# One fetch moved ahead of two others on the loading queue of a fused attention and expert layer

## The reference, cut to what matters

```
x (64*32, 256) as (latent, batch);  ctx (32, 1601, 256)
n  = layernorm(x)
q  = n @ Wq + bq ;  k = ctx @ Wk + bk ;  v = ctx @ Wv + bv        # cross attention
x  = x + gamma * layernorm(softmax(q @ k.T) @ v + n) + beta
x  = x + attention_2(layernorm(x); w_q, b_q, w_kv, w_out, b_out)  # 16 heads over the latents
h  = layernorm(x)
x  = x + sum over the top 2 of 16 experts (gate, up, down) + shared expert
```

## Time and profile before

| | |
|---|---|
| three timed runs | 533.95, 536.94, 537.23 us, median 536.94 |
| the profiled execution | 534.44 us, its span in the trace 532.3 us |
| TensorE busy | 494.5 us (93% of the span) |
| VectorE busy | 386.8 us (73%) |
| ScalarE, GpSimd busy | 219.3 us (41%), 203.7 us (38%) |
| mean granted TensorE clock | 0.984 of full speed |
| DMA traffic | 108.92 MB, mean 205 GB/s |

### The profile page before, as it was taken

How to read it: one execution, slowest core, us unless ns; L and a number is a source line. 1 busy time by engine, 2 the same in 40 slices (tenths; PEclk the granted TensorE clock), 3 DMA queues, 4 the chain that set the end, 5 groups by cost and what they waited for, 6 DMA issues and landing times.

```text
span 532.3 us, 14494 instructions
## 1 busy us (share of the span) xinstructions
PE 494.5 (93%) x5028; PEld 345.4 (65%) x5029; DVE 386.8 (73%) x1053; ACT 219.3 (41%) x656; POOL 203.7 (38%) x344
## 2 busy tenths in 40 slices
PE   7999969999999999999989999999998979999990
PEld 6866536665666656666655667766654548888870
DVE  4897489999789978898743478898766605555764
ACT  3444404533334444344432356666540025555520
POOL 5002130312211221222221476776776625665550
PEclk9999979999999999999999999999999989999997
DMA  8986968686998878885303899720022235555748
GB/s 290 377 313 175 364 195 279 194 265 227 339 299 298 285 232 270 277 273 204 112 21 107 245 309 325 238 90 1 33 75 86 90 109 150 155 158 141 239 100 246
DMA packets 67610, 108.92 MB, mean 205 GB/s; under 512 B 8371, under 2 KB 49381, under 8 KB 67560
## 3 DMA queue, kind: packets, MB, share of 16 engines
q1 hardware_dynamic: 60872, 97.57, 58.1%
q0 software_dynamic: 3792, 8.43, 4.5%
q10 hardware_dynamic: 2896, 2.23, 1.3%
HBM read 85.31 MB, written 24.85 MB: 207 GB/s over the span
## 4 chain that ended last, share of the span: by engine, by line
PE 71%; DMA 9%; DVE 6%; POOL 5%; issue 3%; SPq 2%; ACT 2%; ACTq 1%; POOLq 0%; DVEq 0%
PE banks L1206 15%; PE banks L1180 15%; PE banks L1590 8%; POOL rows_by_expert L773 4%; PE banks L1602 4%; PE banks L1194 3%; PE banks L1219 3%; DMA ring<-in_ctx_dram 3%; PE banks L1584 2%; DMA bk_col<-in_L_xattn_bk_dram 2%; PE banks L1317 2%; PE banks L1369 2%; PE banks L1227 2%; PE banks L1324 2%; PE banks L1340 1%
## 5 line engine op out<-in xcount | busy, mean ns | idle before, releaser
L1714 DVE STREAM_TRANSPOSE ctxT<-ring 128x832 f32<-128x832 f32 x124 | 118.2, 1009 | 8.8 <-DMA ring<-in_ctx_dram 8.5
L1180 PE MATMUL banks<-ctxT,qT_all 32*64 32x416 f32 (+2 forms) x2048 | 96.3, 507 | 6.3 <-DVE ctxT L1714 4.7
L1206 PE MATMUL banks<-ring,prob 128*64 128x256 f32 (+1 forms) x832 | 93.6, 381 | 0.7 <-ACT prob L888 0.7
L1180 PEld LDWEIGHTS banks<-ctxT,qT_all 32*64 32x64 f32 x2048 | 56.4, 133 | 37.0 <-issue 13.1
L1206 PEld LDWEIGHTS banks<-ring,prob 128*64 128x64 f32 (+1 forms) x832 | 58.6, 137 | 31.5 <-issue 4.2
L672 POOL TENSOR_TENSOR var<-mv,eps 128x1 f32<-128x1 f32 x32 | 6.2, 193 | 151.6 <-DVE mv L1755 97.1
L807 POOL DMA_INDIRECT expert_out<-prob,dest x47 | 46.3, 985 | 39.6 <-issue 21.6
L1590 PE MATMUL banks<-ring,ctxT 128*128 x188 | 49.4, 386 | 0.0
L901 ACT ACTIVATE prob<-banks,negmax 128x416 f32<-128x416 f32 (+2 forms) x80 | 41.0, 532 | 19.5 <-DVE negmax L1736 19.5
L1726 DVE TENSOR_REDUCE blockmax<-banks 128x1 f32<-128x416 f32 (+1 forms) x64 | 32.3, 566 | 20.5 <-PE banks L1180 20.5
L720 POOL TENSOR_TENSOR ctxT<-ctxT,k_mask 128x1088 f32<-128x1088 f32 x16 | 33.1, 2069 | 24.9 <-ACT ctxT L997 24.9
(11 more groups left out here) (279 smaller groups left out, 957.0 us busy)
## 6 DMA issues: line engine op xcount, KB each, us to landing
ring<-in_ctx_dram SPq DMA_DIRECT2D x48, 1024.0 KB, 8.5
qT_all<-q_by_pair SPq DMA_DIRECT2D x56, 128.0 KB, 8.0
rows_by_expert<-blank SPq DMA_DIRECT2D x8, 774.0 KB, 6.8
ctxT<-rows_by_expert SPq DMA_DIRECT2D x47, 129.0 KB, 2.1
mid<-stage SPq DMA_DIRECT2D x30, 128.0 KB, 2.3
ring<-in_ctx_dram SPq DMA_DIRECT2D x16, 130.0 KB
ctxT<-mid SPq DMA_DIRECT2D x16, 128.0 KB, 3.8
qT_all<-mid SPq DMA_DIRECT2D x16, 128.0 KB, 4.5
```

Source lines behind the costliest of these rows:

```text
L1180: last = pe.matmul(S[a][64 * b:64 * b + 64, 0:KW[a]], q_rep[mine, r, c, 64 * b:64 * b + 64], ctxT[mine, c, b, 0:KW[a]], start=c == 0, stop ...
L1206: last = pe.matmul(U[64 * b:64 * b + 64, 0:D], probT[0:rows, k, 64 * b:64 * b + 64], ring[0:rows, r, b, k, :], start=k == 0, stop=k == KT)
L1714: dve.transpose(ctxT[:, c].rearrange("p b (k j) -> p (b k) j", j=Q), ring[:, r].rearrange("p b k c -> p (b k) c")[:, :, columns(c):columns ...
```

## The change

Three things are written differently on SyncE's queue, and nothing on another engine. For pair 3, `follow` now issues the context before the queries (`late=0`; the number says which of the two semaphores `q_stored` the queries wait for). The six vector loads, which stood ahead of `follow` of pair 3, stand behind it. `follow` of pair 4 is as it was.

```diff
             load_q(DIRECT, DIRECT)
-            for to, of in ((bv_b, "L0_xattn_bv"), (gamma_b, "L0_xattn_gamma"), (beta_b, "L0_xattn_beta")):
-                sp.dma_start(to[:, :], t[of].partition_broadcast(P)).then_inc(weights_loaded, 16)
-            sp.dma_start(bq2_col[:, :], t["L0_attn_b_q"].rearrange("(p a) -> p a", a=1)).then_inc(weights_loaded, 16)
-            sp.dma_start(bout_b[:, :], t["L0_attn_b_out"].partition_broadcast(P)).then_inc(weights_loaded, 16)
-            sp.dma_start(rbias_b[:, :], t["L0_ffn_router_bias"].partition_broadcast(P)).then_inc(weights_loaded, 16)
-            def follow(i, r, stores=True, late=False):
+            def follow(i, r, stores=True, late=None):
 
                 sp.wait_ge(block_used, (i - RING + 1) * BLOCKS)
-                if not late:
+                if late is None:
                     load_q(i, r)
                 if stores:
                     store(i - RING - 2)
                 for g in range(len(KPARTS)):
                     sp.wait_ge(pv_done, (i - RING) * len(KPARTS) + (g + 1))
                     load_part(i, r, g)
-                if late:
-                    sp.wait_ge(q_stored[1], 16 * QUADS)
+                if late is not None:
+                    sp.wait_ge(q_stored[late], 16 * QUADS)
                     load_q(i, r)
 
-            follow(RING, 0, stores=False)
-            follow(RING + 1, 1, stores=False, late=True)
+            follow(RING, 0, stores=False, late=0)
+            for to, of in ((bv_b, "L0_xattn_bv"), (gamma_b, "L0_xattn_gamma"), (beta_b, "L0_xattn_beta")):
+                sp.dma_start(to[:, :], t[of].partition_broadcast(P)).then_inc(weights_loaded, 16)
+            ...
+            follow(RING + 1, 1, stores=False, late=1)
```

More of the change, by code:

```diff
@@ L500, in follow @@
                     load_part(i, r, g)
-                if late:
-                    sp.wait_ge(q_stored[1], 16 * QUADS)
+                if late is not None:
+                    sp.wait_ge(q_stored[late], 16 * QUADS)
                     load_q(i, r)
-            follow(RING, 0, stores=False)
-            follow(RING + 1, 1, stores=False, late=True)
+            follow(RING, 0, stores=False, late=0)
+            for to, of in ((bv_b, "L0_xattn_bv"), (gamma_b, "L0_xattn_gamma"), (beta_b, "L0_xattn_beta")):
+                sp.dma_start(to[:, :], t[of].partition_broadcast(P)).then_inc(weights_loaded, 16)
+            sp.dma_start(bq2_col[:, :], t["L0_attn_b_q"].rearrange("(p a) -> p a", a=1)).then_inc(weights_loaded, 16)
+            sp.dma_start(bout_b[:, :], t["L0_attn_b_out"].partition_broadcast(P)).then_inc(weights_loaded, 16)
+            sp.dma_start(rbias_b[:, :], t["L0_ffn_router_bias"].partition_broadcast(P)).then_inc(weights_loaded, 16)
+            follow(RING + 1, 1, stores=False, late=1)
             for i in range(RING + 2, 8):
```

## The result

The changed kernel takes 530.96 us (median of 20 runs, 528.96 to 534.85), the kernel before in the same rounds 536.58 us (532.63 to 537.65). The ratio is 0.9921, with a 95% interval of 0.9902 to 0.9941, so 4.2 us less. The means of the 20 and 20 executions differ by 4.6 us (531.4 against 536.0) and the medians by 5.6 us: each kernel's times spread unevenly over 5 to 6 us, which moves a median more than the ratio, and I go by the ratio. On another chip the same file measured 0.9933 (0.9903 to 0.9962), where one execution of ten (539.94 us) was in the chip's slower state and is left out. The forecast was 528.8 us and 6.8 us less: the direction and the place were right, the size was 1.6 times what the ratio shows. The forecast gave 0.55 to a gain of over 1% and 0.41 to one within 1%; at 0.8% the second came.

What follows compares the result with a forecast made beforehand. Pair 3's late context was taken to stall VectorE, then TensorE. Gain of 7.1 us less 0.3 for thin cover, 6.8 net, from the 535.6 us mean gave 528.8 us; 80% range 526 to 534.

Steps and rivals of the forecast that it cites:

- Steps 1 and 2: Pair 3's context on SyncE's queue: first part issued at 41.41, 5.67 us earlier, and landing at 55.3 us.
- step 2: Landing of pair 3's context: 3.28 MB plus 0.9 MB at 356 GB/s, 11.7 us, queries dropped from the traffic ahead.
- Step 3: Pair 3's scores on TensorE end at 70.8 instead of 77.88: 7.1 us gained, 4.7 stall and 2.2 slow clock.
- Steps 4 and 5: Transfers moved behind: vectors land at 59.8, free for pair 3's scores up to 60.3; 0.3 us charged for thin cover.
- step 4: Moved transfers: queries land by 56.8 at no cost; vectors cost 3.0 us of full DMA time and land at 59.8.
- Step 6: What is late next: pair 4's context, issued at 58.28 as before, wanted at 73.5, all traffic ended by about 72.
- third rival: The next stage gives it back: pair 4's queries come at 84.3, 4 us lost, gain 2.8, 532.8 us; chance 0.08.
- vectors late: Vectors queue behind 3.8 MB and land at 62 to 66; gain 3.4 us at 64, 532.2 us; chance 0.23.
- v + 10.5: End of pair 3's scores if the vectors land at time v and GpSimd's additions hold them; free up to v = 60.3.
- Context late: Pair 3's transfers land at 57.3 to 62; at 60 the gain is 4.4 us, 531.2 us; chance 0.09.
- slower: Vectors so late that TensorE, VectorE and GpSimd stand; with pair 4's context ahead, v = 69.0 and 537.2 us; chance 0.05.

Runs made afterwards that it cites:

- vec_only: Kernel before with only the six vector loads moved behind pair 3's context, pair 3's queries still ahead of it; ratio 0.9906 against the kernel before.
- awake: Kernel before, SyncE's order unchanged, with 20 extra 128x128 matmuls on TensorE between the fifth and sixth score blocks of pair 3; ratio 0.9984.
- big_behind: Kernel before with only the four 128 KB vector loads behind pair 3's context, the two small-row loads still ahead; ratio 0.9920.
- small_behind: Kernel before with only the two small-row loads (bq2_col, router bias) behind pair 3's context, the four 128 KB loads ahead; ratio 0.9996.
- five_too: Changed kernel with pair 5's context also issued ahead of the store of pair 0 and pair 5's queries; ratio 0.9894 against the kernel before.

## Why the prediction was right, and where it was too large

**Steps 1 and 2** held. The context landed 14.0 us after its first issue (42.64 to 56.67); step 2 had 13.9. The working was less good than the sum, and that the two agree to 0.1 us is partly luck: the rate of 413 GB/s ended at 52 us, by when 3.6 MB had moved since 42 us (362 GB/s), that is 3.1 MB beside pair 2's queries, and the landing of the 3.28 MB came only at 56.67. What kept it back is not shown. The 0.9 MB of step 2 are in the trace of before: from 62.5 to 72 us it has 2.90 MB in all, 0.52 of them the store that ScalarE's queue began at 62.12, so about 0.9 of pair 4's 3.28 MB had moved when pair 3's context landed. That the last of several DMA engines lagged was my reading; no trace shows them singly. Step 2's price for the queries, which it dropped from the traffic, was not borne out by vec_only.

**Step 3** held: 70.8 forecast for the end of pair 3's scores, 71.50 measured on a run that was 0.5 us late from the start. Its split was 4.7 of stall and 2.2 of clock. The 2.2 of clock is the 4.44 us that blocks 5 to 7 took at a granted clock of 0.50, less 2.2 us, three fifths of the 3.72 us of the five blocks ahead; that was an estimate, and no run shows it. awake puts the clock at 1.8: behind such a stall the three blocks take 2.6 us at a granted clock of 1.00 too, near VectorE's pace of 2.88 us for its three blocks.

**Steps 4 and 5** held to 0.4 us: vectors at 60.15 for a forecast of 59.8 and a limit of 60.3. VectorE did stand for GpSimd, 0.46 us, and TensorE did not notice. The price was off by its parts: queries and vectors, with the rest of the context, kept the DMA engines at share 1.07 for 6 us (52 to 58), where step 4 had 1.5 + 3.0 us, but they began 3 us sooner than it had it. The two errors nearly cancelled, which is luck.

**Step 6 is the term that was mis-sized**: 0 in the sum, 2.2 us measured (1.54 of gap in pair 5's scores, the rest in three blocks that take 2.78 us at VectorE's pace). It followed pair 4's context only. The third rival had the place: "pair 5's context stands behind them". But it priced pair 4's queries, which came in time, and gave the case a chance of 0.08. The row for its start was there. Pair 4's queries waited until 72.34 for a store that does not move with TensorE. In the kernel before that cost nothing: the queue was free at 75.94, and the next transfer, the store of pair 0, waited until 81.18 for ScalarE's rows, which do move with TensorE. In the changed kernel the queries filled the queue from 73.35 to 77.35, the store followed at 77.40 without a wait, and pair 5's context could only come behind it. So SyncE issued it only 3.8 us sooner (82.41 before, 78.62 after) while VectorE asked for it 6.4 us sooner (from 95.9 to 89.5). Before there were 13.5 us from that issue to the need, and the transfer took 13.0 to 14.3 us in the six traces in which VectorE stood for it: next to no slack was left. (`block_used` is no part of this: it stands for the scores of pair i-3, not i-2 as the description of `follow` has it; pair 5's queries were issued by 75.94, before pair 3's scores ended at 77.88.) 6.8 less 2.2 is 4.6, which is what the count at pair 6 (4.7, 4.9) and the two ratios (4.2 and 3.6 us, to 5.2 at the interval's edge) show.

The rivals: *vectors late* did not occur, but at 60.15 the vectors came within 0.15 us of the stated threshold of 60.3. This run stood 0.5 us late from the start, and by v + 10.5 against the measured end of 71.50 its own threshold was 61.0, so some 0.8 us were left. *Context late* and *slower* did not occur.

## What to carry to other kernels

When a stall goes, list every later transfer with the event that releases it, and mark those whose release does not move along: they are the next stall, by the difference. Here it was the next but one fetch. When a transfer is moved past others, price each one passed, stores above all, by who waits for it to finish; in the traces the same edit at pair 5 was worth 2.5 and 2.0 us with the store in place, and nothing with the store passed.

## What the runs showed of the hardware that I had not expected

Four loads of 128 KB that copy one row of 1 KB to 128 partitions held back a 3.2 MB fetch issued after them by about 3.4 us (15.5 us from first issue to landing, 12.1 with different source rows, 12.1 in big_behind too). Two loads of 4-byte and 64-byte rows, which I had suspected as much, held back nothing that can be measured (small_behind, 0.9996). The landing of a 3.2 MB fetch came some 4 us after nearly as many bytes had passed: in the changed kernel the rate of 413 GB/s ended at 52 us, and VectorE was released at 56.67. And behind gaps of the same 1.54 us TensorE's granted clock stayed at 1.00 in the changed kernel (2.78 us for the three blocks) and fell to 0.50 in five_too (3.91 us).
